# Layer-1 neighbour sum by accumulating scatters into eight DRAM copies, with one edge sort instead of two

## The reference

```
layer 0: attention over edges, grouped by dst (softmax of q[s]*k[d], weighted sum of x[s])
         + linear attention over all nodes, layer norm, mlp, layer norm; then a routed ffn
layer 1: support = layer_norm(x)
         out[src[e]] += edge_weight[e] * support[dst[e]]     for every edge e
         x += out @ W + b
         + linear attention, merge, norms, mlp; then two routed experts
```

## Time and profile before

| what | value |
|---|---|
| median of the runs shown | 7841.31 us |
| profiled execution, first to last instruction | 7837.5 us, 121180 instructions |
| PE / DVE / ACT / POOL busy | 4906.9 / 3746.0 / 1981.3 / 4885.1 us |
| two sorts | 0 to 266.5 us |
| `sums0` (first attention sums) | 297.0 to 716.1 us |
| `gat_` (layer-0 edges) | 1251 to 3266 us |
| `gcn_` (layer-1 edges), with the clearing of its sum | 5136 to 7153 us |
| software queue (POOL's DMAs) | 432.72 MB, 20.1% of 16 engines |

### The profile page before, as it was taken

The page is one execution under the profiler, slowest core; times in us unless marked ns, Lnnn a source line. Parts: engine busy times, 40 slices in busy tenths (PEclk is TensorE's granted clock), DMA queues, the critical chain, the costliest instruction groups (busy, mean ns, idle before and its releaser), DMA issues. The chain is left out here.

```text
span 7837.5 us, 121180 instructions
## 1 busy us (share of the span) xinstructions
PE 4906.9 (63%) x21606; PEld 3530.6 (45%) x21607; DVE 3746.0 (48%) x11942; ACT 1981.3 (25%) x4749; POOL 4885.1 (62%) x5920
## 2 busy tenths in 40 slices
PE   0365354889999999619834549235555555665692
PEld 0133342556666666418712438224444443444582
DVE  7896526666677777631121330353333333333314
ACT  0221152445555555305322213000000000001351
POOL 0002767777777777667747767777777777773002
PEclk9987676999999999859967879678877878778796
DMA  2100002444444444200010000023333333331000
GB/s 83 47 0 10 4 7 66 116 116 116 116 116 116 116 116 116 67 15 3 3 37 3 6 12 3 3 74 105 106 106 106 105 106 106 106 106 51 12 0 34
DMA packets 542397, 496.32 MB, mean 63 GB/s; under 512 B 411923, under 2 KB 438923, under 8 KB 541579
## 3 DMA queue, kind: packets, MB, share of 16 engines
q0 software_dynamic: 200192, 432.72, 20.1%
q1 hardware_dynamic: 215435, 57.63, 3.4%
q10 hardware_dynamic: 126720, 5.46, 1.1%
HBM read 465.14 MB, written 30.23 MB: 63 GB/s over the span
## 5 line engine op out<-in xcount | busy, mean ns | idle before, releaser
L999 POOL DMA_INDIRECT XN<-table,XN x3128 | 2986.9, 955 | 832.0 <-issue 705.5
L425 POOL DMA_INDIRECT records<-slot_rec,slot_pos x1564 | 1545.3, 988 | 457.1 <-issue 456.8
L1313 PE MATMUL gcn_psE<-XN,gcn_pE 128*125 x3520 | 1164.7, 491 | 1035.8 <-SPq L979 1026.2
L1313 PEld LDWEIGHTS gcn_psE<-XN,gcn_pE 128*125 128x125 f32 x3520 | 816.3, 242 | 1384.1 <-issue 1233.4
L1133 PE MATMUL gat_psE<-XN,gat_pE 128*125 x3520 | 882.2, 394 | 3.4 <-ACT gat_pE L1186 2.9
L1341 DVE TENSOR_TENSOR room<-room,gcn_psE 125x256 f32 x440 | 185.3, 421 | 1193.5 <-PE gcn_psE L1313 1192.7
L73 POOL TENSOR_TENSOR cell<-cell 1x1 int32<-1x1 int32 x1006 | 189.9, 189 | 856.1 <-DMA slot_pos<-spill_pos 808.3
L1133 PEld LDWEIGHTS gat_psE<-XN,gat_pE 128*125 128x125 f32 x3520 | 638.1, 191 | 85.8 <-issue 4.6
L541 ACT ACTIVATE gcn_w_stage<-room 125x512 f32 (+1 forms) x25 | 15.6, 622 | 2083.3 <-PEq L115 2083.3
L1329 DVE TENSOR_SCALAR gcn_pE<-iota_n,gcn_lk,gcn_rec 128x125 f32<-128x125 f32 x1760 | 505.4, 359 | 16.0
L478 POOL TENSOR_TENSOR X<-X,room x150 | 124.8, 866 | 607.8 <-DVE room L520 604.6
(11 more groups left out here) (358 smaller groups left out, 7678.9 us busy)
## 6 DMA issues: line engine op xcount, KB each, us to landing
XN<-table,XN POOLq DMA_INDIRECT x3128, 2.8
records<-slot_rec,slot_pos POOLq DMA_INDIRECT x1564, 2.1
XN<-records SPq DMA_DIRECT2D x782, 6.0 KB
table<-XN SPq DMA_DIRECT2D x10, 1250.0 KB
gat_rec<-records ACTq DMA_DIRECT2D x440, 6.0 KB
gcn_rec<-records ACTq DMA_DIRECT2D x440, 6.0 KB
X<-in_x SPq DMA_DIRECT2D x1, 6250.0 KB
out_x<-X SPq DMA_DIRECT2D x5, 1250.0 KB
```

The source lines that it names most:

```text
L425: pool.indirect_dma_start(out=rec_d[self.which], out_offset=bass.IndirectOffsetOnAxis(ap=slot_pos[:, h, j:j + 1], axis=0), in_=slot_rec[:, ...
L999: pool.indirect_dma_start(out=rows_t[:, s, j, :], out_offset=None, in_=table, in_offset=bass.IndirectOffsetOnAxis(ap=rec_g[:, s, j, 1:2].b ...
L1313: last = pe.matmul(psE[d][0:B, 0:D], pE[:, d, j, :], rows_t[:, slot_of(g), j, :].rearrange("p a w -> p (a w)"), start=(j == 0), stop=(j == ...
```

## The change

The layer-1 sum is turned round. Instead of sorting by `src` and gathering the rows of `dst`, it keeps the order by `dst` of the first sort, so that the rows to be read lie in one block of `XN` in SBUF, and adds the weighted rows into DRAM at `src`:

- `sort_edges` runs once. It builds a second table of steps, by tiles of 128 edges (1613 tiles, padded to 1616 = 404 quads of 4), clears eight DRAM copies `acc` of 6400 x 256 floats (6.55 MB each) from a zero tile, and also loads `X`.
- All `Mover` calls with `turns`, the place computation in `sums0`, `spill_pos[1]` and `table1` with its stores go away.
- `push_rows` replaces `edge_sums`. For each quad PE transposes the sources (L1336), DVE marks equal sources within a tile (L1435) and finds for every edge whether another one of its tile carries its sum (L1442 to L1447; the others go to a trash row), DVE builds one-hot targets (L1423), PE forms the mixing matrix (L1347) and multiplies it with a block of `XN` (L1358), ACT copies both results (L1381, L1389), and POOL sends four indirect DMAs of 128 rows of 1 KB that add into four of the eight copies (L1473). POOL waits before a quad until the quad two back has landed.
- `collect_rows` then reads all eight copies back and adds them on DVE.

```diff
-        for which, (k_, o_) in enumerate((("dst", "src"), ("src", "dst"))):
-            sort_edges(which, A[k_], A[o_], A["edge_weight"])
-            end_phase()
+        sort_edges(A["dst"], A["src"], A["edge_weight"])
+        end_phase()
...
+                        sp.wait_ge(zero_set, 1)
+                        for dst in acc:
+                            sp.dma_start(dst.rearrange("(p r) d -> p r d", p=P),
+                                         zeros[:, :].unsqueeze(1).broadcast_to([P, NACC // P, D])).then_inc(cleared, 16)
                         sp.wait_ge(rec_done, 1)
...
+                        sp.dma_start(X[:, :, :], rows(A["x"])).then_inc(x_in, 16)
...
+                        sp.wait_ge(cleared, 16 * COPIES)
...
-                        mv.sp(sp)
...
-                        mv.pool(pool)
...
-                            if edge:
-                                places.blocks(k * 2, 2)
...
+                        def body(t, s):
+                            k = t * RG + s
+                            pool.wait_ge(m_done, k + 1)
+                            pool.wait_ge(idx_done, k + 1)
+                            if not early(t, s, 2):
+                                pool.wait_ge(added_rows[s % 2], (t * (RG // 2) + s // 2) * (16 * QUAD))
+                            settle(pool, cell[0:1, 0:1], settled, k)
+                            for j in range(QUAD):
+                                pool.indirect_dma_start(
+                                    out=acc[s % 2 * QUAD + j], out_offset=bass.IndirectOffsetOnAxis(ap=idx[:, s, j:j + 1], axis=0),
+                                    in_=rows_t[:, s, j, :], in_offset=None, compute_op=ALU.add).then_inc(added_rows[s % 2], 16)
...
+                        def messages(t, s):
...
+                            for j in range(QUAD):
+                                b = pe.value_load(tile_blk[0:1, bass.ds(k * QUAD + j, 1)], min_val=0, max_val=NB - 1)
+                                last = pe.matmul(psM[d][j // 2][:, (j % 2) * D:(j % 2 + 1) * D], mix[:, d, j * P:(j + 1) * P],
+                                                 one(XN[0:B, bass.ds(b, 1), :]), start=True, stop=True)
...
+        def collect_rows():
...
+                    for r in (slice(0, 112), slice(112, B)):
+                        eng.dma_start(dst[r, i * n:(i + 1) * n, :], rows(src[0:N, :])[r, i * n:(i + 1) * n, :]).then_inc(ready, 16)
...
+                        for i in range(5):
+                            halves(sp, U, acc[0], i, arrived[i])
+                            halves(sp, XN, acc[1], i, arrived[i])
+                        for j in range(2, COPIES):
+                            for i in range(5):
+                                sp.wait_ge(summed, (j - 2) * 5 + i + 1)
+                                halves(sp, XN, acc[j], i, arrived[i])
```

More of the change, by code:

```diff
@@ L34 @@
 NS = NG + NB - 1
+NT = EP // P
+TS = NT + NB - 1
+QUAD = 4
+NQ = -(-TS // QUAD)
+TP = NQ * QUAD
+COPIES = 8
+NACC = 6400
+NOBLK = 1000.0
 RING = 8
@@ L136, in gps_kernel @@
     table0 = nc.dram_tensor("table0", [N, D + SMALL], F32).ap()
[L137 to L141, removed]
+    acc = [nc.dram_tensor(f"acc{i}", [NACC, D], F32).ap() for i in range(COPIES)]
+    spill_rec = nc.dram_tensor("spill_rec", [P, EC, RW], F32).ap()
+    spill_pos = nc.dram_tensor("spill_pos", [P, EC], I32).ap()
+    rec_d = nc.dram_tensor("records", [EP, RW], F32).ap()
+    tile_blk_d = nc.dram_tensor("tile_blk", [1, TP], I32).ap()
+    tile_blkf_d = nc.dram_tensor("tile_blkf", [P, TP], BF16).ap()
     with ctx:
@@ L344, in _ @@
[L344 to L358, removed]
+                        st(dve.tensor_copy(step_grp[:, :], iota_s[0:1, :]))
@@ L395, in gps_kernel @@
-        class Mover:
[L400 to L403, removed]
-                    self.filled = [sem(f"{name}_filled{h}") for h in range(2)]
-                    self.settled = sem(name + "_settled")
+                        pe.wait_ge(tiles_bnd, 1)
+                        for i in range(4):
+                            w = min(512, TP - i * 512)
+                            last = pe.matmul(psT[i][:, 0:w], ones[0:NB - 1, :], ge_t[0:NB - 1, i * 512:i * 512 + w], start=True, stop=True)
@@ new lines, in take_rows @@
+                        def take_rows(t, s):
+                            k, d = t * RG + s, s % 2
+                            act.wait_ge(m_mm, k + 1)
+                            if not early(t, s, RG):
+                                act.wait_ge(added_rows[s % 2], (t * (RG // 2) + s // 2 - 1) * (16 * QUAD))
+                            for h in range(2):
+                                last = act.activation(rows_t[:, s, 2 * h:2 * h + 2, :].rearrange("p s d -> p (s d)"), psM[d][h][:, :], ACT.Copy)
+                            last.then_inc(m_done, 1)
@@ new lines, in hots @@
+                        def hots(t, s):
+                            k, d = t * RG + s, s % 2
+                            if not early(t, s, 2):
+                                dve.wait_ge(a_mm, k - 1)
+                            for j in range(QUAD):
+                                last = dve.tensor_scalar(hot[:, d, j, :], iota_n[:, :], lk[:, d, j:j + 1], rec_t[:, s, j, 2:3],
+                                                         ALU.is_equal, ALU.mult)
+                            last.then_inc(hot_done, 1)
@@ new lines, in body @@
+                        def body(t, s):
+                            same(t, s)
+                            if at(t, s, 1):
+                                places(*at(t, s, 1))
+                                hots_next = at(t, s, 1)
+                            targets(t, s)
+                            if at(t, s, 1):
+                                hots(*hots_next)
+                        places(0, 0)
+                        st.all()
+                        hots(0, 0)
+                        quads(dve, body, st, RG * 5)
@@ L1348, in route_rows @@
+        def route_rows(selw):
             name = "topk"
```

483 lines of the change are left out of this document (283 added, 200 removed).

## The result

| | before | after |
|---|---|---|
| median, us (range, runs) | 7840.12 (7838.11 to 7847.16, 4) | 8419.9 (8405.01 to 8428.34, 4) |
| profiled execution: span, us | 7837.5 | 8426.6 |

The changed kernel is slower: ratio 1.0737, interval 1.0722 to 1.0753. The forecast was 7475, 945 us less. The sign is wrong, and the time lies 220 us above the range (7340 to 8200).

The account below looks back on a forecast made before the run. POOL was taken to bound the layer-1 edge stage. 7837.5 - 476 (movers) - 155 (`sums0` places) - 44 (one sort) + 309 (scatters and collecting) = 7471.5, so 7475 as median; range 7340 to 8200 us.

Parts of the forecast that it names:

- where the trace is silent: Price of an adding scatter in the layer-1 edge stage: bounds 5.09 to 8.8 us a quad; the lower end was taken.
- 5.3 us a quad: Layer-1 scatters: 5.1 us of POOL plus 0.2 for DVE's work beside it; 404 quads make 2141 us.
- Collecting: `collect_rows`: reading back 51.2 MB in 1 KB rows at 23.6 GB/s an engine takes 139 us, 150 with ends.
- Break-even: Layer-1 scatters: the savings are lost when a quad reaches 6.2 us, 1.55 us a scatter.
- A's lowest prices: Four points of the 75% chance of a faster kernel, taken from the case where POOL pays for the second source.
- Rival A: Layer-1 scatters: POOL pays for the second source, 1.43 to 1.91 us each, quad 6.9 to 8.8, total 8150 or 8890; 25%.
- its sign: Evidence that POOL pays for the second source: the scatter line L1473 above 1.25 us each.
- Rival B: Layer-1 scatters: adding is slow on the transfer engines or in landing, above 6.4 us; quad 5.7, total 7640; 15%.
- Rival C: Layer-1 edge stage: PE becomes the bound at its lower clock, quad 6.8, total 8080, or 7780 half the time; 10%.
- Parts 1 to 3: Before the layer-1 scatters: movers gone, -476 us; places gone from `sums0`, -155; one sort with eight copies cleared, -44.
- The 9.2 us for a chunk of `sums0`: PE's time per chunk of `sums0` without waiting for DVE; 9.6 was taken for 25 chunks, 240 us.
- The new wait: Layer-1 scatters: POOL waits until the quad two back has landed; 6.4 us lie between, gathers landed in 3.1, so hidden.

Follow-up runs that it names:

- first three groups: Runs on three chips, one group each, where the unedited kernel before took 10400, 10283 and 10384 us; on the last two groups' chips it took 7842 and 7836.
- third group: Runs on one chip; its kernel before, unedited, was executed for its trace and took 10377.9 us.
- second group: Runs on one chip; its changed kernel, run again unedited, took 9229.0 us, 0.8972 of the kernel before there.

## Why the prediction was wrong, point by point

- **The step that failed** is the choice between the bounds in "where the trace is silent": "it seems to go by rows, not by what is done with them". It is the other way round: 64 rows fewer save 0.07 to 0.09 us, adding costs 0.58. Why adding costs POOL this stays open. The earlier trace rows showed two DMAs of 128 rows each, so they could not tell a price for rows from one for the DMA, and neither of them added, so they said nothing about adding. The sum was 5.3 us a quad where 7.43 stood: (7.43 - 5.3) x 404 = 861.
- **Collecting** was mis-sized: 217 us for 150, 67 more. I had carried the 23.6 GB/s of each of five engines over to sixteen. Together 928 of the 945 us missed.
- **Break-even** held: 6.2 us a quad, 1.55 us a scatter with its issue of 0.30 (1.25 on L1473's row). The quad is 1.23 above it; 1.23 x 404 = 497, and 67 of collecting, make 7840 + 564 = 8404 for 8420. It lay in the lower third of the bounds, 5.09 to 8.8 us a quad, and their middle, 6.95, was already on the slower side. Taking the lower end turned a question that the trace left open into a chance of 50% for one answer. The chances also hold a slip: "4 (A's lowest prices)" counts as faster, but A begins at 6.9 us a quad, above the 6.2 of the break-even, so by its own terms none of A is faster.
- **Rival A** is what happened, at a price between its two, 1.56 for 1.43 to 1.91, and with its sign (L1473 above 1.25). Its own formula gives 7475 + 861 = 8336, with the 67 of collecting 8403. Its mechanism is not shown as I put it: a third address for each row would be paid by the row, but of the 0.58 us added at 128 rows, 0.55 are there at 64 (1.466 - 0.915) and, carried on, about 0.52 at none. I gave it 25% for a near equality that did not bear on it.
- **Rival B** was half right without effect: a row takes the engines about three times as long (0.67 x 16 x 7.43 us / 512 = 156 ns, records included, for 51 ns of a plain one, 0.31 x 16 x 5.24 / 512), and 512 such rows are 5.0 us of all sixteen engines, below POOL's pace and even below my 5.3. Landing took 3.8 us, not above 6.4. From the Trainium skill's rule of two reads for a reducing transfer (Collectives: The Full Stack, The bandwidth ceiling) I had worked out a share of 0.75 at 5.3 us a quad; the trace has 0.67 at 7.43. That is three times the engine time of a plain row, where the rule makes it twice.
- **Rival C** did not decide: the clock is 0.81 as feared, but PE stands idle for 36% of the window.
- **Parts 1 to 3** held: 666 for 675 in the traces, 777 for 763 when done alone. The 9.2 us for a chunk of `sums0` is 9.0 by its own terms (7.06 + 1.2 + 0.75); the 9.6 that the sum used hides the slip.
- **The new wait** of POOL is hidden, as said; even one of half the distance is.

## What to carry to other kernels

Where an engine that issues DMAs is the bound, count its DMAs by kind and price each kind by itself: here an indirect DMA cost POOL 0.98 us and one that adds 1.56, almost whatever its rows and bytes. If the one price that decides does not stand in the trace, near equalities between other kinds do not bound it: spread the chances over all that lies between the bounds, and state the break-even in the same unit as the row, so that it is plain which prices lie on which side. A change can hold a part that gains (777 us here, from sorting once) and a part that pays for it (the scatters, without which sorting once gives another sum than the reference's); price each by itself.

## What the runs showed of the hardware

The same kernels took very different times on different chips, and the order of the two turned round. On the chips of the first three groups the stages in which POOL issues plain indirect DMAs are longer, and no others; the kernel before is that of the third group, the kernel after that of the second:

| stage, us | before | before, third group | after | after, second group |
|---|---|---|---|---|
| `ln_c` to `ln_d` (gathers) | 2147 | 3027 | 2124 | 2947 |
| `ln_d` to `ln_e` (mover before, none after) | 662 | 1075 | 517 | 517 |
| `ln_f` to `ln_g` (mover before, none after) | 464 | 760 | 354 | 354 |
| `ln_g` to `ln_h` (gathers before, adding scatters after) | 2219 | 2575 | 3472 | 3473 |
| `ln_h` to `ln_i` (no POOL DMA) | 445 | 447 | 445 | 444 |

The window of the kernel before there, for the second row:

```profile
2000.00:3000.00 1000.00, 767.36 (x3328) 506.23 (x3328) 475.40 (x2116) 358.24 (x1058) 554.19 (x696) 0.84 0.33 82
```

and the two waits that sum to most in it. ACT and POOL stand still for nothing that the profile shows, up to 6.8 and 1.7 us at once, where the same waits last at most 1.8 and 0.3 us in the kernel before of the result:

```profile
ACT XN L1171 <- issue: 304.4, 150, 6.8
POOL XN L999 <- issue: 184.7, 521, 1.7
```

> The kernel before itself, for its trace beside the others. On two chips it took 10400 and 10283 us instead of 7840, the changed kernel on the second 9229 instead of 8420. Theory F (on these chips an engine pauses when its loop comes to instructions that must be fetched again, and nothing covers the pauses where an engine other than POOL sets the pace or POOL's own pauses add to its work): against the trace of before shown, both edge stages are longer (the first by 800 us, as in the changed kernel), every single operation is as long as before, and the pauses stand at the same places of each turn of the loops. Rival (slower DMA engines or DRAM): a gather, a landing or a transfer takes longer. On a chip of the first kind: 7840 and no pauses.

It took 10377.9 us. A gather cost POOL 0.953 us there too, so slower DMA work of POOL is excluded. So are slower transfer engines: the packets of POOL's queue took 20.1% of 7837.5 us in the kernel before of the result and 15.3% of 10376.2 here, 1575 and 1588 us of the sixteen engines. Both edge stages are longer, the first by 880 us, the second by 356. Stages with the adding scatters do not change, and slack does not hide pauses in them: DVE, ACT and PE wait in mid-stage for at most 4.7, 5.1 and 3.4 us on either kind of chip. That is why the changed kernel, which replaces 1564 gathers and 1564 plain scatters by 1616 adding ones, is 7% slower on one kind of chip and 10% faster on the other. What makes the engines pause is open; the runs with 64 rows, which bear on it too, were on a chip without pauses. The Trainium skill (Runtime: NRT & Kernel Launch, Instruction fetch mechanics) says that a taken branch out of the instructions an engine holds stalls it until they are fetched; the loops of the edge stages would be a place for that, and no run here shows whether it is the cause. The traces do not speak for it: the page's queues for instructions hold 38 and 12 packets in the kernel before on both kinds of chip, though whether they hold every such fetch is not known.
